# Feed-forward of a per-sample linear and a block-diagonal MLP: from four groups of eight units to eight groups of four

## What is computed

```python
t = einsum('bsi,boi->bso', x, weight[adapter_ids])     # 1024 x 1024 weights, one of 16 for each sample
t = t.reshape(b * l, 1024)[:, perm].reshape(b * l, 16, 64)
t = einsum('bhd,hdm->bhm', t, up)                      # 64 -> 256 in each head
t = gelu(t)
t = einsum('bhm,hmd->bhd', t, down)                    # 256 -> 64 in each head
out = x + t.reshape(b * l, 1024)[:, argsort(perm)]
```

## Time and profile before

| | us |
|---|---|
| median of 3 runs | 291.43 |
| lowest and highest | 291.36 and 291.61 |
| the profiled execution: its own time | 290.92 |
| its span, first to last instruction | 289.1 |
| PE busy in it | 283.6 (98%) |
| ACT, DVE, POOL busy | 161.7, 198.9, 98.3 |

### The profile page before, as it was taken

The page is one execution under the profiler, slowest core; times in us unless marked ns, Lnnn a source line. Parts: engine busy times, 40 slices in busy tenths (PEclk is TensorE's granted clock), DMA queues, the critical chain, the costliest instruction groups (busy, mean ns, idle before and its releaser), DMA issues.

```text
span 289.1 us, 4341 instructions
## 1 busy us (share of the span) xinstructions
PE 283.6 (98%) x1694; PEld 216.4 (75%) x1694; DVE 198.9 (69%) x227; ACT 161.7 (56%) x179; POOL 98.3 (34%) x96
## 2 busy tenths in 40 slices
PE   7999999999999999999999999999999999999994
PEld 7889888888988988888898898883376358338531
DVE  3698778669669689788778787362954675395333
ACT  5655454355245258338328333399579939948930
POOL 2000000008877001730000244075677773362054
PEclk9999999999999999999999999999999999999999
DMA  6999999799999999999998577555357743132033
GB/s 209 367 379 418 374 366 400 274 396 350 399 423 409 409 407 376 335 407 379 285 314 274 160 251 244 195 169 163 147 167 205 210 182 145 65 119 109 2 145 145
DMA packets 23795, 77.87 MB, mean 269 GB/s; under 512 B 2784, under 2 KB 11360, under 8 KB 18912
## 3 DMA queue, kind: packets, MB, share of 16 engines
q1 hardware_dynamic: 7056, 43.39, 39.9%
q0 software_dynamic: 7584, 25.18, 25.2%
q10 hardware_dynamic: 9136, 9.05, 9.0%
HBM read 60.82 MB, written 16.78 MB: 268 GB/s over the span
## 4 chain that ended last, share of the span: by engine, by line
PE 96%; DMA 1%; POOL 1%; SPq 1%; issue 0%; DVE 0%; ACT 0%; POOLq 0%; DVEq 0%
PE ps L577 38%; PE ps L583 20%; PE ps L635 19%; PE ps L611 5%; PE ps L614 5%; PE ps L617 5%; PE ps L553 3%; PE ps L558 1%; DMA w_raw<-w 1%; POOL out_rows L287 1%; SPq L199 1%; DVE w_raw L476 0%; ACT w_hi L375 0%; POOLq L307 0%; SPq L227 0%
## 5 line engine op out<-in xcount | busy, mean ns | idle before, releaser
L577 PE MATMUL ps<-x_pair,w_hi 128*128 128x512 f32 x480 | 114.5, 391 | 0.0
L327 ACT ACTIVATE w_hi<-w_raw 128x1024 fp32r<-128x1024 f32 x58 | 58.3, 1054 | 81.1 <-PE ps L583 45.9
L577 PEld LDWEIGHTS ps<-x_pair,w_hi 128*128 128x128 f32 x480 | 88.2, 188 | 17.1
L433 DVE TENSOR_TENSOR w_lo<-w_raw,w_hi 128x1024 fp32r<-128x1024 f32 x60 | 71.0, 1222 | 17.1 <-ACT w_hi L327 16.3
L269 POOL DMA_INDIRECT t_raw<-y_rows,idx x32 | 35.6, 1112 | 96.4 <-DMA y_rows<-y_out 80.0
L583 PEld LDWEIGHTS ps<-x_pair,w_lo 128*128 128x128 f32 x480 | 61.5, 191 | 2.3
L583 PE MATMUL ps<-x_pair,w_lo 128*128 128x256 f32 x480 | 62.3, 283 | 0.0
L356 ACT ACTIVATE hidden<-ps 128x1024 f32<-128x1024 f32 x48 | 47.0, 1024 | 21.7 <-PE ps L617 20.1
L635 PE MATMUL ps<-hidden,down_sb 128*64 128x512 f32 (+1 forms) x264 | 55.8, 581 | 0.0
L462 DVE TENSOR_REDUCE y_out<-ps 128x256 f32<-128x512 f32 x64 | 42.6, 685 | 14.7 <-PE ps L583 14.5
L635 PEld LDWEIGHTS ps<-hidden,down_sb 128*64 128x64 f32 x264 | 18.6, 137 | 35.5 <-issue 29.4
(11 more groups left out here) (29 smaller groups left out, 152.7 us busy)
## 6 DMA issues: line engine op xcount, KB each, us to landing
w_raw<-w SPq DMA_DIRECT2D x29, 1024.0 KB, 8.2
y_rows<-y_out ACTq DMA_DIRECT2D x32, 256.0 KB, 7.3
x_raw<-x_cols SPq DMA_DIRECT2D x7, 1024.0 KB, 8.3
w_raw<-w SPq DMA_DIRECT2D x4, 256.0 KB, 4.1
w_raw<-w SPq DMA_DIRECT2D x2, 512.0 KB, 7.6
t_raw<-up SPq DMA_DIRECT2D x1, 1024.0 KB, 11.4
down_sb<-down SPq DMA_DIRECT2D x1, 1024.0 KB, 12.9
w_raw<-w SPq DMA_DIRECT2D x2, 384.0 KB, 6.2
```

What stands on the lines that cost most here:

```text
L327: nc.scalar.activation(w_hi[:, g % WS, k, :], w_raw[:, g % WRAW, k, :], ACT.Copy).then_inc(w_hi_done, 1)
L433: nc.vector.tensor_tensor(w_lo[:, g % WS, k, :], w_raw[:, g % WRAW, k, :], w_hi[:, g % WS, k, :].bitcast(F32), ALU.subtract).then_inc(w_lo ...
L577: nc.tensor.matmul(y_bank(g, o), w_hi[:, ws, k, col], x_pair[:, xs, k, :, :], start=(k == 0), stop=False)
```

## The change

The groups become half as large and twice as many: `GROUP` 4, eight groups of eight up halves and four down units. Down unit i has tile `ps[i]` to itself and uses its first bank. `COPIED` has one half of the eight (h = 2), so ACT does seven Gelus from PSUM and one in place in each group. `hidden` has four slots. The `t_high` and `t_low` of a group are now those of two groups ahead (the same eight units ahead as before), so that the first eight units are still prepared ahead of the feed-forward. The second token part of the very last unit goes to the second bank of `ps[0]`. The counts in the waits follow.

```diff
-YS, TG, SS, HS, XR = 4, 16, 8, 8, 10
+YS, TG, SS, HS, XR = 4, 16, 8, 4, 10
-GROUP = 8
+GROUP = 4
-COPIED = (2, 5, 8, 11)
+COPIED = (2,)
         def down_place(f, n):
             if n == 1:
-                return ps[0][:, 0, 0:S]
-            return ps[f % GROUP // 2][:, f % 2, :][:, token_parts(f)[0]]
+                return ps[0][:, 1, 0:S]
+            return ps[f % GROUP][:, 0, :][:, token_parts(f)[0]]
...
                 for f in range(GROUP * j, GROUP * (j + 1)):
                     scatter(f)
-                if j == 0:
+                if j == 1:
                     for f in range(XR, LATE):
                         gather_rows(f)
...
-                        pe.wait_ge(added, GROUP * (j - 1) + 2 * (h + 1))
+                        pe.wait_ge(added, GROUP * (j - 1) + h + 1)
...
-                if i % 2 == 0:
-                    up_banks_free(j, PARTS - BANKS + i // 2)
+                up_banks_free(j, PARTS - BANKS + i)
```

More of the change, by code:

```diff
@@ L50 @@
 WRAW, WS, XS = 4, 2, 2
-YS, TG, SS, HS, XR = 4, 16, 8, 8, 10
+YS, TG, SS, HS, XR = 4, 16, 8, 4, 10
 PAIR, BANKS = 2, 4
-GROUP = 8
+GROUP = 4
 GROUPS = NF // GROUP
 PARTS = GROUP * MT
-COPIED = (2, 5, 8, 11)
-GELU_PLACE = {0: 0, 1: 1, 3: 2, 4: 3, 6: 4, 7: 5, 9: 6, 10: 7, 12: 8, 2: 9, 13: 10, 5: 11, 14: 12, 15: 13, 8: 14, 11: 15}
+COPIED = (2,)
+GELU_PLACE = {0: 0, 1: 1, 3: 2, 4: 3, 2: 4, 5: 5, 6: 6, 7: 7}
 UP_UNITS = (16, 17)
@@ L402, in _ @@
                     t_high((g - T_FROM) // 2)
-            t_high(GROUP - 1)
+            t_high(2 * GROUP - 1)
             for j in range(GROUPS):
@@ L411, in _ @@
                 gelu(j, 4)
+                gelu_in_place(j, 2)
+                gelu(j, 5)
                 gelu(j, 6)
                 gelu(j, 7)
[L414 to L425, removed]
+                if j + 2 < GROUPS:
+                    for f in range(GROUP * (j + 2), GROUP * (j + 3)):
                         t_high(f)
@@ L511, in _ @@
                 if g == NL - 2:
-                    t_low(GROUP - 1)
+                    t_low(2 * GROUP - 1)
             for j in range(GROUPS):
@@ L517, in _ @@
                 first = GROUP * j
-                if j + 1 == GROUPS:
-                    for f in range(first, NF):
+                if j + 2 >= GROUPS:
+                    for f in range(first, first + GROUP):
                         add_x(f)
@@ L522, in _ @@
                     add_x(first)
+                    t_low(first + 2 * GROUP)
                     add_x(first + 1)
+                    t_low(first + 2 * GROUP + 1)
+                    t_low(first + 2 * GROUP + 2)
                     add_x(first + 2)
-                    t_low(first + GROUP)
+                    t_low(first + 2 * GROUP + 3)
                     add_x(first + 3)
[L527 to L537, removed]
         @block.tensor
```

## The result

The changed kernel takes 292.81 us (median of 16 runs, 292.21 to 294.0) against 291.36 us (16 runs). The ratio is 1.0054, 95% interval 1.0046 to 1.0062: slower by 1.45 us. Forecast were 292.9 us and +1.5 us. In a later set of runs on another chip the ratio was 1.0055 (1.0035 to 1.0074). Two executions of all, of 311.28 us and 312.06 us with a lower granted clock than their neighbours, are left out of the ratios.

What follows compares the result with a forecast made beforehand. PE, busy 98% of the span, was taken to bound the kernel. Four more turns each way at 4 x 0.38 = 1.5 us, with all waits met, gave 291.43 + 1.5 = 292.9 us; range 292.1 to 294.2 (8 in 10).

Steps and rivals of the forecast that it cites:

- The turns, 4 x 0.38: Feed-forward on PE: four more turns each way between up and down matmuls, 0.38 us per group, 1.5 us in all.
- The estimate from the Trainium skill: Turns on PE: two drains a group at some 166 ns each, 0.33 us, would sum to 1.3 us instead of 1.5.
- PE meets every wait: Short group in the feed-forward: all results PE needs come in time, so the group lasts 12.69 us.
- The narrowest place, 0.13 us: Down unit 1: Gelu 5 ends at 6.87 us of the group, its weights load at 7.00, 0.13 us to spare.
- rival 2: Down unit 1: ACT late; 0.2 to 0.4 us a group would give 294.5 to 296.1 us; chance 0.09.
- Rival 1: Turn to up: PE waits for DVE's t_lo, which the new order removes, giving 291.4 us, not slower; chance 0.08.
- Rival 3: Add 10: gathered rows of unit 10 come late, 1.9 us once, 294.8 us; chance 0.03.
- Rival 4: Change not doing what it says: given nothing; 0.02 left for an unseen gain such as faster down units.
- The tail and the start: First and last units: run as before, tail the same; span of the profiled execution 289.1 to 290.6 us.

Runs made afterwards that it cites:

- extra pairs: Kernel before plus up-form fp32r matmul pairs between down units of each group: one pair 1.0086, two pairs 1.0171.
- fp32 pair: Kernel before plus one plain fp32 matmul pair in the up form, in front of half 8 of each group: 1.0111.
- pair at the head: Kernel before plus one up-form fp32r matmul pair ahead of down unit 0 of each group, so no turn is added: 1.0018.
- Gelu 6 first: Changed kernel with the Gelus of halves 5 and 6 in the other order on ACT: 1.0017 on the kernel before.
- shared tiles: Changed kernel with two down units sharing a tile, as before the change, in groups of four: 1.0054 on the kernel before.
- `t_high` first: Changed kernel with one t_high ahead of Gelu 5 on ACT in the six groups that have any: 0.9938 on the kernel before.

## Why the prediction was right

- *The turns, 4 x 0.38.* Right in mechanism and size. 0.37 us a group after; 12.68 us for 12.69. The extra pairs show that it is the turn (0.32 to 0.35 by itself) and that it adds up (2 x 0.58). The fp32 pair leaves at most 0.05 for the type, so it is the layout, by elimination. The rest up to 0.38 isn't separated; a pair at the head of the down units cost 0.03 more than its own 0.227.
- *The estimate from the Trainium skill* ("TensorEngine Tiling (Array Packing)", Tiling Modes: a change of mode drains TensorE; two drains with the constant of "TensorE: Matmul & The Clock Gate", Single matmul latency, 0.33 us a group). The experiments agree in size: 0.32 to 0.35. That what passes in this time is a drain no row shows, and the page gives its constant for one bf16 matmul alone. The 0.38 read from the period, 0.37 after, gave the measured sum better.
- *PE meets every wait.* Right. In the trace after, the half starts, the Gelus, the first down unit and the last add lie within 0.05 us of the group as written out. Gelu 5 starts 5.82 us after the group's start (255.16 - 249.34; written 5.85), and add 3 ends 13.55 after it (262.20 + 0.69 - 249.34; written 13.56):

```profile
255.16 2.85 ACT L356 ACTIVATE hidden<-ps 128x1024 f32<-128x1024 f32 x3
```

```profile
262.20 0.69 DVE L468 TENSOR_TENSOR w_raw<-ps,w_raw 128x512 f32<-128x512 f32 x1
```

- *The narrowest place, 0.13 us.* Mis-sized. I took the weight load a pair ahead as the moment at which the wait is due. It can be late without loss; about 0.5 us were there. That rival 2 did not happen was therefore less of a near thing than I said, and by that its 0.09 was high.
- *Rival 1, a wait for `t_lo`.* Falls twice: the extra pair turns without such a wait, and in the trace after, where `t_lo` comes two groups ahead, the same 0.81 us of PEld at the same turn are put down to nothing:

```profile
249.34 0.18 PEld L595 LDWEIGHTS ps<-t_hi,up_hi 64*128 64x128 f32 x2 [0.81 <-issue]
```

  The name in the bracket of the earlier trace rows was that of the semaphore that came last, 0.54 us before.
- *Rival 3, late rows.* Did not happen: no gap in PE's row, and moving five of the gathers away gained nothing.
- *Rival 4, faster down units.* Did not happen: the down stretch of four units, 7.02 us, is that of eight, 13.89, less four units of 1.717.
- *The tail and the start.* The tail was as before. The start moved by 0.76 us in the profiled execution, which the sum for it (290.6 us of span) did not allow for; the medians are not touched by it.

## What to carry to other kernels

Where PE alternates between matmuls that split the array by rows and by columns, count the turns: each round trip cost 0.32 to 0.38 us here, whatever the length of the stretches. As far as turns go, longer groups are better, and halving the groups is paid by as many more turns; groups of more than eight were not tried. A short group stays at that price only if each engine's results are in time. That could be written out here from starts and durations of a trace to within 0.05 us; what was misjudged, by 0.4 us, is the moment at which PE needs a result. A wait that PE meets late cost more than its length: behind a stop of 0.13 us the next half took 0.12 us longer, and behind one of 0.39 us (Gelu 6 first) the group was 0.44 longer.

## What the runs showed that was not expected

*A restart costs by itself.* In the kernel with shared tiles PE stopped for 0.13 us without any turn, and the half behind it took 0.80 us in place of 0.68. The first half behind a turn has the same 0.12. In both cases the weights are not loaded ahead: the load stands at the very start of the half, as here at 261.22:

```profile
261.22 0.19 PEld L595 LDWEIGHTS ps<-t_hi,up_hi 64*128 64x128 f32 x2 [0.40 <-DVE w_raw L468]
```

That the late load is what costs, and so a part of the price of a turn, is likely but not shown: in the kernel with `t_high` first a load as late, without a stop, cost no more than the 0.07 us of its whole group.

*On some chips engines stand still in one stretch.* In two sets of runs, on two chips, the kernel before took 303.4 us, in the others 291.0 to 291.4. All eight kernels traced in those two sets lose their time between about 216 and 240 us; elsewhere only the first group of three of them is longer, by 0.3 to 0.4 us. In the kernel with the pair at the head, PE (first halves of the matmuls), DVE, and a window (columns: stretch, length, busy time of PE, PEld, DVE, ACT, POOL, granted clock, share of DMA, GB/s):

```profile
221.92 0.79 PE L611 MATMUL ps<-t_hi,up_hi 64*128 64x512 f32 x2 [1.80 <-issue]
...
225.06 0.79 PE L611 MATMUL ps<-t_hi,up_hi 64*128 64x512 f32 x2 [1.49 <-issue]
```

```profile
223.69 1.22 DVE L467 COPY hidden<-ps 128x1024 f32<-128x1024 f32 x1 [7.33 <-PE ps L617]
```

```profile
220.00:225.00 5.00, 1.77 (x8) 0.83 (x6) 1.22 (x1) 1.02 (x1) 3.78 (x5) 0.67 0.76 216
225.00:230.00 5.00, 2.62 (x10) 1.72 (x12) 1.23 (x1) 2.05 (x3) 2.13 (x3) 0.50 0.44 116
230.00:235.00 5.00, 5.00 (x28) 2.77 (x26) 0.05 (x1) 5.00 (x6) 2.27 (x3) 0.80 0.60 165
```

PE is busy 4.4 of the first 10 us, but it is not PE that stands first. DVE's copy at 223.69 is that of half 8, which PE had begun at 216.09 and which was ready some 0.9 us later; DVE stood 7.33 us, most of it with this work in front of it. ACT stands in the same way. PE's half at 225.06 wants the tile that this copy empties, and starts 0.15 us behind the copy's end (224.91); the others of the stretch start 0.06 to 0.15 us behind a late Gelu. GpSimd issues its gathers one behind another until 225.6; ACT and DVE go on at 227.95 and 228.10. On the other chips PE is busy all the time in this stretch, with the same gathers.

The clock adds to it. PE was busy 1.0 of the 4.3 us before 221.9, where its granted clock fell from full (2.4 GHz) to 0.50 (1.2 GHz); it stayed there for some 10 us, until 232.0, when PE had been at work since 229.03 again. PE was busy 6.2 us at this level, so by an estimate from that some 3 of the 11.0 us lost go to the clock.

Against their undisturbed periods the kernels with groups of eight lost 12.4, 11.0, 11.4 and 11.4 us there, the three with groups of four 10.7, 7.0 and 8.2 us, and that with groups of two 9.5. What holds ACT and DVE up was not found: the kernels with fewer gathers in that place were made to tell, and met a chip without it. Nor was the changed kernel itself run on such a chip. Its nearest relatives there were 0.9938 (`t_high` first, so faster than the kernel before), 1.0017 (Gelu 6 first, no clear difference) and 1.0054 (shared tiles, slower), though each of them has a handicap of its own. If the changed kernel loses over 1.5 us less than the kernel before does, it is not slower on such chips; this is open. The price of the turns, in the groups outside the stretch, is the same in all traces.
